# Grouped attention: class ends turned by TensorE, register averages scaled by ScalarE, class rows sent straight to the first two units

## What is computed

```
q, k, v = x @ W_qkv                       # per head, 8 channels each
sim = mean over heads of cosine(q[5:], g) # one number per token
sim = (sim - sim.min()) / (sim.max() - sim.min())
pos = sim > 0.9                           # the class of each token
x_pos = softmax(q k^T * scale, keys: registers and pos) v
x_neg = softmax(q k^T * scale, keys: registers and not pos) v
out = for token 5..511: x_pos where pos, else x_neg
      for the 5 registers: (x_pos + x_neg) * 0.5
x = x + out @ W_proj + b_proj
```

## Time and profile before

| what | us |
|---|---|
| median of 3 runs | 1236.61 (1233.19 to 1239.44) |
| the profiled execution | 1231.52 |
| its span, first to last instruction | 1229.8 |
| PE, DVE, ACT, POOL busy | 1101.3, 805.6, 738.4, 346.0 |
| mean granted clock of TensorE, share of full | 0.965 |

### The profile page before, as it was taken

One profiled execution on the slowest core, in us unless ns is written; L12 is line 12 of the kernel. 1 busy time (PEld: TensorE's weight loads), 2 busy tenths in 40 slices (PEclk: granted clock), 3 DMA queues, 4 the chain that ended last, 5 costly groups with the idle time before them and its releaser, 6 DMA issues. The chain is left out here.

```text
span 1229.8 us, 35580 instructions
## 1 busy us (share of the span) xinstructions
PE 1101.3 (90%) x14748; PEld 561.8 (46%) x14748; DVE 805.6 (66%) x1311; ACT 738.4 (60%) x1460; POOL 346.0 (28%) x673
## 2 busy tenths in 40 slices
PE   6999888888899997789999999999978786899996
PEld 2344443333234442456767666767645333222221
DVE  4897558777633233177777767776726456999984
ACT  5314627777554444366676676676644372799994
POOL 0552203333235344144224224322204424100000
PEclk9999959999999999799999999999999997999999
DMA  5000171111053300521121120100100004311100
GB/s 196 1 0 1 29 229 45 51 42 30 4 136 69 68 1 0 149 28 11 9 16 10 10 17 8 11 8 7 13 5 1 1 19 138 132 42 43 42 17 35
DMA packets 134479, 51.61 MB, mean 42 GB/s; under 512 B 103904, under 2 KB 126448, under 8 KB 133680
## 3 DMA queue, kind: packets, MB, share of 16 engines
q1 hardware_dynamic: 134284, 49.32, 17.0%
q10 hardware_dynamic: 36, 0.02, 0.0%
HBM read 33.12 MB, written 15.81 MB: 40 GB/s over the span
## 5 line engine op out<-in xcount | busy, mean ns | idle before, releaser
L2370 DVE TENSOR_REDUCE re_nmax<-ps 128x1 f32<-128x512 f32 x256 | 159.0, 684 | 88.3 <-PE ps L2138 88.3
L2281 ACT ACTIVATE normed<-ps,re_nmax 128x512 f32<-128x512 f32 x256 | 159.0, 688 | 89.7 <-DVE re_nmax L2370 89.7
L2159 PE MATMUL ps<-const,normed 128*128 128x128 f32 x1024 | 145.8, 281 | 7.8 <-ACT normed L2281 4.8
L1191 DVE TENSOR_REDUCE ga_nmax<-ps 128x2 f32<-128x1024 f32 x128 | 147.0, 1217 | 3.3 <-PE ps L947 3.3
L1095 ACT ACTIVATE ga_pt<-ps 128x512 f32<-128x512 f32 x256 | 139.2, 598 | 15.6 <-PE ps L983 14.5
L2159 PEld LDWEIGHTS ps<-const,normed 128*128 128x128 f32 x1024 | 108.8, 141 | 38.4 <-ACT normed L2281 27.2
L1191 DVE TENSOR_REDUCE da_nmax<-ps 128x2 f32<-128x256 f32 (+3 forms) x128 | 102.3, 820 | 35.8 <-PE ps L958 34.7
L1095 ACT ACTIVATE da_pt<-ps 128x512 f32<-128x512 f32 (+3 forms) x256 | 96.9, 435 | 44.3 <-PE ps L983 42.1
L1621 DVE TENSOR_TENSOR ex_u<-ps,ex_s 128x512 f32<-128x512 f32 x48 | 32.8, 690 | 98.7 <-PE ps L1486 75.8
L2287 ACT ACTIVATE re_pT<-ps 128x512 f32<-128x512 f32 x128 | 76.4, 597 | 29.1 <-PE ps L2159 20.3
L2390 DVE COPY re_pT<-ps 128x512 f32<-128x512 f32 x128 | 82.3, 685 | 11.5 <-PE ps L2159 10.7
(11 more groups left out here) (396 smaller groups left out, 1988.2 us busy)
## 6 DMA issues: line engine op xcount, KB each, us to landing
ex_gates<-gates_scratch SPq DMA_DIRECT2D x4, 2048.0 KB, 14.8
da_qst<-da_stacks SPq DMA_DIRECT2D x32, 96.0 KB, 2.2
da_kst<-da_stacks SPq DMA_DIRECT2D x32, 96.0 KB, 2.3
ga_qst<-ga_stacks SPq DMA_DIRECT2D x32, 96.0 KB
ga_kst<-ga_stacks SPq DMA_DIRECT2D x32, 96.0 KB
da_stacks<-da_qkparts SPq DMA_DIRECT2D x6, 384.0 KB, 3.4
ga_stacks<-ga_qkparts SPq DMA_DIRECT2D x6, 384.0 KB, 2.9
weights<-in_weights SPq DMA_DIRECT2D x1, 2048.0 KB, 8.0
```

The lines of the kernel that those rows point to most:

```text
L1191: nc.vector.tensor_reduce(nmax[:, u % 2, :, pr, qt], g.ps[:, 2 * (step % S_GROUPS):2 * (step % S_GROUPS) + 2, 0:keys_of(qt)], AX.X, ALU.ma ...
L2159: last = nc.tensor.transpose(g.ps[:, bank_of("tile", s, idx), bass.ts(kt, 128)], p[:, QUAD_ORDER[idx], bass.ts(kt, 128)], g.c("ident"))
L2281: nc.scalar.activation(p[:, QUAD_ORDER[idx], :], g.ps[:, S_BANK + QUAD_ORDER[idx], :], ACT.Exp, bias=nmax[:, s % 2, idx:idx + 1]).then_inc ...
L2370: nc.vector.tensor_reduce(nmax[:, s % 2, idx:idx + 1], g.ps[:, S_BANK + quad, :], AX.X, ALU.max, negate=True).then_inc(maxed, 1)
```

## The change

Seven edits, all in this part:

- The copy to `gr_sim` goes; the reduces and the scaling read PSUM.
- The maximum over partitions: VectorE widens the two ends to 128 equal columns each, TensorE turns both (two 128x128 transposes into bank 1, behind the V matmuls of batch 1), VectorE reduces the two groups of 128. GpSimd's instruction goes.
- `copy_key(2)` and `copy_key(3)` now stand ahead of the reduces.
- The four averages of the registers move from GpSimd to ScalarE, behind the four exponentials.
- The last two reciprocals of the sums stand ahead of VectorE's main loop, which they followed into before.
- SyncE: the class rows of units 0 and 1 come straight from `rows` in SBUF, 8 DMAs each in place of 4; the store to DRAM comes behind them, and the wait for it ahead of unit 2.
- SyncE: `write_parts(1)`, `(2)` and `(3)` stand each ahead of `load_maxima(1)`, `(2)` and `(3)`, where all three stood ahead of the first.

The diff, cut to its core:

```
@@ attention_stage
-            LOADS = 4 + (4 if classes else 0)
+            DIRECT = 2
+
+            def loads(u):
+                return 0 if u < 0 else loads(u - NBUF) + 4 + ((8 if u < DIRECT else 4) if front else 0)
...
                         for s, stack in enumerate((qst, kst)):
                             for par in range(2):
-                                sp.dma_start(stack[64 * par + TERM_ROWS:64 * par + KS, at, :, :],
-                                             classes[2 * s:2 * s + 2, b, :].unsqueeze(1).broadcast_to([2, 2, T]))\
-                                    .then_inc(stack_loaded[at], 16)
+                                to = stack[64 * par + TERM_ROWS:64 * par + KS, at, :, :]
+                                if u < DIRECT:
+                                    for pr in range(2):
+                                        sp.dma_start(to[:, pr, :], front.class_rows(b, s)).then_inc(stack_loaded[at], 16)
+                                else:
+                                    sp.dma_start(to, classes[2 * s:2 * s + 2, b, :].unsqueeze(1)
+                                                 .broadcast_to([2, 2, T])).then_inc(stack_loaded[at], 16)
...
                     load_stack(0)
                     if front:
-                        front.store_classes(sp)
+                        sp.wait_ge(front.rows_made, 6)
+                        load_classes(0)
                     write_quad(2)
                     load_stack(1)
                     if front:
-                        front.wait_stored(sp)
-                        load_classes(0)
                         load_classes(1)
+                        front.store_classes(sp)
                     write_quad(3)
                     for u in range(2, NBUF):
                         load_stack(u)
-                        if classes:
+                        if front:
+                            if u == DIRECT:
+                                front.wait_stored(sp)
                             load_classes(u)
-                    for b in range(1, B):
-                        write_parts(b)
                     for u in range(1, QUADS):
+                        if u < B:
+                            write_parts(u)
                         load_maxima(u)
...
@@ grouped_front.tensor
             last.then_inc(self.v_made, 1)
+            if b == 1:
+                pe.wait_ge(self.widened, 1)
+                for n in range(2):
+                    last = nc.tensor.transpose(g.ps[:, 1, bass.ts(n, 128)], self.ends_wide[:, n, :], g.c("ident"))
+                last.then_inc(self.ends_turned, 1)
...
@@ grouped_front.scalar
+        for b in range(B):
+            act.wait_ge(self.inverted, b + 1)
+            nc.scalar.activation(self.p[:, b, :], self.p[:, b, :], ACT.Identity, scale=self.total[:, b:b + 1])\
+                .then_inc(self.averaged, 1)
...
@@ grouped_front.vector
         divide(3)
+        copy_key(2)
+        copy_key(3)
         dve.wait_ge(self.compared, 1)
...
-        nc.vector.tensor_copy(sim[:, :], g.ps[:, 0, :]).then_inc(self.ended, 1)
-        dve.wait_ge(self.ended, 1)
...
-        copy_key(2)
+        nc.vector.tensor_reduce(self.ends[:, 0:1], g.ps[:, 0, REG:T], AX.X, ALU.min, negate=True)\
+            .then_inc(self.ended, 1)
+        nc.vector.tensor_reduce(self.ends[:, 1:2], g.ps[:, 0, REG:T], AX.X, ALU.max).then_inc(self.ended, 1)
+        dve.wait_ge(self.ended, 2)
+        nc.vector.tensor_copy(self.ends_wide[:, :, :], self.ends[:, :].unsqueeze(2).broadcast_to([128, 2, 128]))\
+            .then_inc(self.widened, 1)
+        dve.wait_ge(self.ends_turned, 1)
+        nc.vector.tensor_reduce(ends_all[:, :], g.ps[:, 1, 0:256].rearrange("p (n k) -> p n k", n=2), AX.X, ALU.max)\
+            .then_inc(self.gathered, 1)
...
-        copy_key(3)
...
+        invert(B - 2)
+        invert(B - 1)
...
@@ grouped_front.gpsimd
-        pool.wait_ge(self.ended, 3)
-        nc.gpsimd.partition_all_reduce(self.ends_all[:, :], self.ends[:, :], 128, bass.bass_isa.ReduceOp.max)\
-            .then_inc(self.gathered, 1)
...
-            pool.wait_ge(self.inverted, b + 1)
-            nc.gpsimd.tensor_scalar(self.p[:, b, :], self.p[:, b, :], self.total[:, b:b + 1], None, ALU.mult)\
-                .then_inc(self.averaged, 1)
```

23 lines of the change are left out of this document (10 added, 13 removed).

## The result

| | changed kernel, median us | kernel before | ratio (95% interval) | difference, us |
|---|---|---|---|---|
| first set | 1222.87 of 7 (1220.72 to 1229.39) | 1235.08 of 7 | 0.9918 (0.9893 to 0.9944) | -10.1 |
| second set | 1222.56 of 9 (1219.72 to 1229.93) | 1230.84 of 20 | 0.9933 (0.9910 to 0.9956) | -8.2 |
| third set | 1226.15 of 12 (1221.94 to 1228.69) | 1230.98 of 29 | 0.9961 (0.9946 to 0.9975) | -4.8 |

The last column is the ratio turned into microseconds; the two medians of the first set lie 12.2 us apart, those of the others 8.3 and 4.8. The change makes the kernel faster, by 4.8 to 10.1 us (under 1%), 7.7 as a plain mean of the three. Forecast were 7.3 us and a time of 1229.3 between 1225.0 and 1236.5; the measured 1222.87 of the first set lies outside.

A forecast was written before the change was run, and what follows sets the result against it. VectorE's fixed pace was taken to bound the loop, so the gain was an earlier start, 5.6 us, plus less idling, 1.7: 7.3 us off a median of 1236.6, giving 1229.3, range 1225.0 to 1236.5.

The forecast's parts named there:

- The loop starts 5.6 sooner: Grouped part's main loop: VectorE's first maximum at 1024.0 in place of 1029.62, 5.6 us sooner, bounds 4.9 and 6.3.
- The class rows 3.9 sooner: Ahead of the loop: class rows complete at 1015.5 in place of 1019.35, 3.9 us sooner, by the new maximum's path.
- Which path ends last: At the loop's start: registers, if TensorE is cold, free VectorE at 1024.1, later than SyncE's direct DMAs at 1023.6.
- rival 1: More is gained: TensorE at full clock through scores and first steps, both idle stretches go; 9.1 us, 1227; chance 0.14.
- Direct DMAs 0.6 each: SyncE's queue ahead of the loop: 8 class row DMAs from SBUF at 0.6 us, 4.8 us, issued by 1021.9.
- rival 4: Slower: issuing a direct DMA costs more; gain nought at 1.2 us each, 1244 at 1.69; chance 0.06.
- The averages, 1.7: First steps of the loop: moving averages to ScalarE removes VectorE's 1.67 us idle; 1.7 us gained, bounds 0 and 2.9.
- rival 2: New wait for averages: TensorE's lower clock idles VectorE as before, maxima cost 1.5; gain 4.1 us, 1232.5; chance 0.18.
- The spread, 0: Writes of parts spread over the loop: counted as 0, with 0 to 1.5 us lost as the bound.
- Unit 1 hidden by half a microsecond: Loop, start of unit 1: class rows landed by 1032.7, due 1033.2 on TensorE's side; about two us cover on VectorE.
- Rival 3, SyncE's queue: SyncE's queue sets the loop's start and stacks for units 1 to 3 come late; 0 to 3 us remain, 1235; chance 0.12.
- The two rules: Skill's rules against the change: partition reductions on GpSimd, and copying PSUM to SBUF first; dropped copy saves 0.6 net.

The follow-up runs named there:

- e8: e7 plus matmuls nobody reads: 4 behind the register scores, 2 in each of steps 1 and 2, one in each of steps 13 to 15; 1221.88 us, ratio 0.9926.
- e3: The changed kernel with the writes of batches 1 to 3 put back ahead of the first load of maxima, in both attention stages; ratio 0.9990.
- e7: The changed kernel with unit 0's four direct key rows issued by ScalarE and the last two reciprocals back in VectorE's first two steps; 1222.39 us, ratio 0.9926.
- e4: The changed kernel with matmuls nobody reads: 11 behind the register scores and 2 in each of steps 0 to 2; 1221.74 us, ratio 0.9912.
- e2: The kernel before with only the spread of the writes, one batch ahead of each load of maxima, in both attention stages; ratio 0.9998.
- e10: e8 with two more matmuls nobody reads, put ahead of the register scores; ratio 0.9891.
- e12: The changed kernel with the maximum over partitions back on GpSimd, without widening or transposes; early key copies and ScalarE averages stay; ratio 0.9942.
- e13: The changed kernel with writes all ahead of the first maxima in the first layer's attention, spread in the grouped part alone; 1226.85 us, ratio 0.9965.
- e11: The changed kernel with the class rows of units 0 and 1 through DRAM again, as before the change; ratio 0.9940.
- e14: e10 with unit 1's four direct key rows issued by ScalarE behind the averages; 1219.19 us, ratio 0.9908.

## Why the prediction was right or wrong, point by point

- **The time, outside the range.** 1229.3 was the median of three runs, 1236.6, less 7.3. In the first set the base was 1235.1, 1.5 lower, and the two medians lie 12.2 apart, 4.9 more than 7.3; the interval of the ratio, 6.9 to 13.2 us, still holds 7.3. The medians of the same kernel in the five sets were 1235.1, 1231.8, 1230.8, 1234.9 and 1231.0, their mean 1232.7; those of the changed kernel have a mean of 1223.9. Of the 5.4 us between forecast and that mean, 3.9 are the base and 1.5 the gain. The step that failed is the low end of the range: it was written as a gain of 11.6 from that one base, with no room for the base itself being high, though the profiled execution beside it had 1231.52. That two of the three sets lie below the range and the third, 1226.15, in it is at least in part scatter: the stretch that no edit touches was 3.4 us shorter in the changed kernel's three traces than in those of the kernel before.
- **The loop starts 5.6 sooner: right.** Three traces of either kernel give 21.0 and 15.3, so 5.7. **The class rows 3.9 sooner** were 4.4: widening 0.29 for 0.4, transposes 0.38 for 0.4, reduce 0.43 for 0.4, scaling 0.81 for 0.69.
- **Which path ends last** was wrong, with no harm to the sum. TensorE stayed at full clock over the scores (1.10 us a pair), so the registers were done at 1017.9, 1.1 us ahead of the first step; I had them 0.5 behind the DMAs. 2.5 us of idleness did not lower the clock where 7.59 had: rival 1 in its first half. It was not safe, though: in e8 the same 2.52 us were followed by scores of 1.90 and 1.74 us a pair.
- **Direct DMAs 0.6 each:** 0.64 and 0.60. Right, and rival 4 falls with it. Store and maxima from SBUF were the right neighbours, not the class rows from DRAM at 0.28.
- **The averages, 1.7: the term that failed.** Measured nought: the mean of three loops is 165.4 us before and 165.5 changed. The releaser of the 1.67 was rightly GpSimd: the first turning had waited 1.63 us for its averages, and waits no more. What failed is that I left the clock as it was, since "the turning at step 3 will be no busier than now". Where the clock is low for as long in both (6.8 to 6.9 us), VectorE idles 3.1 and 3.0 us in the first eight steps of the kernel before, and 1.6 and 2.1 in e3 and e7: 0.9 to 1.6 us less. But in the changed kernel's three traces the clock is low for 10.2, 17.1 and 17.1 us, in those of the kernel before for 6.8, 13.7 and 6.9; turnings and values take 1.11 and 2.07, and fill what the averages freed (2.92, 3.24 and 3.24 us in the first eight steps). That is rival 2 in its half on the clock; its other half, maxima late by 1.5, did not come. With filling VectorE idles 0 in these steps (e4).
- **The spread, 0:** true of it alone (e2), and off by the point: without it all of the 8 us are lost (e3). The working for "a step in hand" counted the queue between the maxima and the stacks, but never the 12 us by which the writes begin later against the loop, of which 5.2 reach the maxima. It also read the last twelve writes (7.01 us) and not all eighteen (18.12). Its 1.5 MB of data has no row; no term rests on it.
- **Unit 1 hidden by half a microsecond:** it held, because the loop lost more than that ahead of it. At full pace TensorE waits 1.5 to 1.7 us there (e4, e10), and VectorE 0.3 to 0.5 of it.
- **Rival 3, SyncE's queue:** it was the last to arrive at the loop's start and would have taken all back at unit 1's maxima, but for the spread. As written, with late stacks of units 1 to 3, it did not come.
- **The two rules.** The maximum by GpSimd costs 6.2 us of the start (e12, 21.57 for 15.3), since nothing hides the time around its 0.37 us. The Trainium skill (GPSIMD Engine Reference, 4.1 Engine selection) would leave a reduction along the partition dimension there; by this measurement it is the wrong side for a small one on a chain. Reading PSUM cost nothing for the reduces (0.69) and 0.2 for the scaling (0.81 for 0.59); what the Trainium skill (VectorE: DVE Perf Modes, Rules for kernel authors) would save by copying first is less than the copy's 0.69.
- **"The change touches nothing else"** was wrong: both attention stages share the lines of the spread. That it cost nothing measurable is luck (e13).
- **The sum** was 7.3. The traces of the part give 216.1 before and 210.5 changed, means of three, so 5.6: the start, and nothing beside it. The times give 4.8, 8.2 and 10.1. The 2 us between their mean and the part's are not shown to be the change's: in the traces the difference ahead of the part lies in the stretch that no edit touches (665.6 and 662.2 us), and the equal kernels were up to 2.5 us apart. That 7.3 and 7.7 lie so near is thus partly luck, since a term of 1.7 was missing.
- **The signs.** VectorE's idle time in the loop was to be near 1.2 us for 2.9; it was 2.9 to 5.1. No idle time at the starts of units 1, 2 and 3, no "issue" ahead of the third parts, 8 direct DMAs in 4.9 us: as forecast.

## What to carry to other kernels

Where a chain is shortened, look at TensorE's clock in the first steps of what follows: here it fell in every kernel without filling, with or without a wait ahead, and what another engine's edit frees can be filled by TensorE's slower steps. Filling, with the awaited DMAs split over a second queue, brought 7.0 us more in the one set that has both kernels. When the bound moves forward, lay every queue beside it anew, since one that was ahead can be behind by what was gained plus what was added to it. And take the base of a forecast of an absolute time from all executions at hand, with a range for the base of its own.

## What the runs showed of the hardware

- GpSimd's maximum over partitions takes 0.37 us, but with it stand 5.6 to 5.7 us ahead of it and 7.0 to 7.4 ahead of the next ordinary instruction. The second part, the way back, I had read from the earlier trace rows and not understood as the price of the same instruction: with the maximum gone, the third parts follow at once.
- Executions with a mean granted clock of 0.967 or more and those with 0.963 or less are 5.5 us apart in this kernel (medians 1221.7 and 1227.1), more than most of the edits tried.
- The granted clock fell in the loop's first steps in all thirteen traces without filling (in e11 just ahead of them, while TensorE still waited), whether that step had waited 0.00 us (e2, e12), 0.71 (before), 0.85 (e7) or 2.65 (changed), and stayed low for 3.5 to 17.1 us. With filling there (e4, e8, e10, e14) it stayed at 1.00 over these steps.
- Eighteen writes of 32x3x512 in a row took 11.34 us in e3, 0.63 each, and 18.12 in the kernel before; in the changed kernel six took 3.20 ahead of unit 1's maxima and 2.78 and 4.00 elsewhere, 0.46 to 0.67 each.
